# GpSimd instead of VectorE makes the marks of each edge's column in a four-layer graph network kernel

## The chip, the cores and the metric

The kernel runs on one core of a Trainium2 chip. The metric is the device time of one execution in microseconds (us), without profiling. Before the change it is 4020.64 us, the median of three runs (4017.7 to 4024.07 us). A core has a matrix engine (TensorE, PE in the profile), a vector engine (VectorE, DVE), a scalar engine (ScalarE, ACT), GpSimd (POOL) and SyncE (SP), which here only starts transfers. Each engine works through its own list of instructions in order; they wait for each other by semaphores. Transfers with a list of row numbers (indirect DMAs) are issued by GpSimd.

## The reference

There are 100,000 nodes with 16 features each and 50,000 edges. Four layers follow each other; each normalizes the node features, takes for every edge the features of one of its ends, makes a message of 16 numbers from them, and adds the messages up at the other end:

```python
edge_index = jnp.stack([src, dst])
h = relu(layernorm(x))
x = x + _L0_gnn_ref(h, edge_index, edge_weight, ...)   # message: h[src] * weight; summed at dst
h = relu(layernorm(x))
x = x + _L1_gnn_ref(h, edge_index, edge_attr_2, ...)   # 16 small products, weighted by hat functions
h = relu(layernorm(x))
x = x + _L2_gnn_ref(h, edge_index, edge_attr_8, ...)   # two edge convolutions, one in each direction
h = relu(layernorm(x))
x = x + _L3_gnn_ref(h, edge_attr_8, ...)               # message, sum, and an update of every node
```

Layers 0 and 2 gather by `src` and sum by `dst`; layers 1 and 3 the other way round.

## The kernel before

**Tiles.** A node's number is split in three: its partition (one of 128), its block of 16 columns, and its column in that block. The edges are first sorted by block, once for each of the two directions, and written as records (21 or 13 numbers each) into a table in device memory (`place(0)` and `place(1)`, line 489: 391 indirect transfers each, of 128 edges). A record holds the number of the row to gather, the partition (field `LO`) and the column in the block (field `HI`) of the node that receives the message, and the edge's attributes.

**An edge stage.** Each layer has one edge stage (`edges(l)` in the programs of VectorE and ScalarE). It goes over 55 groups of 8 tiles; a tile is 128 edges, one on each partition. For a group g:

- SyncE fetches the records of the group into `rec[g % 4]` (line 394). For group g + 4 it first waits until VectorE has made `spread` of group g and ScalarE `at_lo` of group g.
- GpSimd waits for the record (`rec_in`) and for the buffer `rows[g % 4]`, then issues 8 indirect transfers, one a tile, which gather 128 rows of 16 features (line 507).
- ScalarE makes from `LO` the 0/1 matrix `at_lo` of each edge's partition (lines 859 and 863).
- VectorE makes the message `raw` (`messages(g)`), partly from products of TensorE. In it `columns(g)` (line 1213) compares the numbers 0 to 15 with field `HI` for all 8 tiles at once: one comparison of 128x128, which leaves a 1 at the edge's column in `at_hi[g % 2]`.
- VectorE multiplies `at_hi` by `raw` into `spread` (line 1218, 128x2048).
- TensorE multiplies `at_lo` by `spread` tile by tile (line 586; in layer 3 line 582). This sums the tile's messages by partition and column.
- VectorE adds tile after tile to a running sum (`run`, line 1238, 8 instructions of 128x256 a group), and SyncE writes the group's 1 MB of running sums to device memory (line 401). `run` of group g - 1 stands behind `spread` of group g.

**Order.** The order on every engine is written out by hand. GpSimd's list is: a few masks, `place(0)`, the 440 gathers of layer 0, `place(1)`, and the 440 gathers of each of layers 1, 2 and 3, then the additions of the last stage, the node update (line 531). Between the edge stages lie node stages, in which the sums are read back and the features normalized; GpSimd waits there for the stored table of features (`store`). The node stage of layer 1 runs on the other engines while GpSimd issues `place(1)`.

**Buffers.** `rec` and `rows` are four deep (`RING`), `at_hi`, `at_lo`, `raw` and `spread` two deep. `iota16` holds the numbers 0 to 15; VectorE makes it once at the start (line 1336).

Of the kernel before, what the change touches and what calls it, by code (L numbers as in the profile page):

```python
# [4 lines left out]
P = 128  # L5
N, E, D = 100000, 50000, 16
# [4 lines left out]
BC = 16  # L11
# [25 lines left out]
G = 8  # L37
GROUPS = T // G
RING = 4
# [25 lines left out]
def build_gnn(nc, x_in, src_in, dst_in, attr2_in, attr8_in, attr8_rev_in, ew_in, w0_in, slw_in, w1_in,  # L65
# [4 lines left out]
    ALU, ACT, AX = mybir.AluOpType, mybir.ActivationFunctionType, mybir.AxisListType  # L70
# [5 lines left out]
    with ctx:  # L76
        def sb(name, shape, dt=f32):
            return ctx.enter_context(nc.sbuf_tensor(name, shape, dt))

        def sem(name):  # L80
            return ctx.enter_context(nc.semaphore(name))
# [14 lines left out]
        iota1 = sb("iota1", [P, P])  # L96
        iota16 = sb("iota16", [P, BC])
# [5 lines left out]
        rec = [sb(f"rec{k}", [P, G * FD]) for k in range(RING)]  # L103
        keep = [sb(f"keep{s}", [P, T]) for s in range(2)]
        last = [sb(f"last{s}", [P, NBS], i32) for s in range(2)]
        small = sb("small", [P, 5 * CH])
        at_hi = [sb(f"at_hi{p}", [P, G * BC]) for p in range(2)]
        hats = [sb(f"hats{p}", [P, G * 8]) for p in range(2)]
        rowmask = sb("rowmask", [P, 8])
        eps = sb("eps", [P, 1])  # L110
# [46 lines left out]
        spread = [work[:, 2048 + i * G * BW:2048 + (i + 1) * G * BW] for i in range(2)]  # L157
# [7 lines left out]
        def late(words):  # L165
# [67 lines left out]
        w4_ready = sem("w4_ready")  # L233
        stored = sem("stored")
        dve_step = sem("dve_step")

        names = ("taken", "outer", "bandT", "bandS", "prod", "used", "preact", "silu", "hats", "hatsraw",
                 "abs", "lo", "spread", "summed", "run")
        lacks = [("outer", "bandT", "bandS", "prod", "used", "preact", "silu", "hats", "hatsraw"),
                 ("taken", "preact", "silu"),  # L240
                 ("taken", "outer", "preact", "silu", "hats", "hatsraw"),
# [4 lines left out]
        rec_in = [sem(f"rec{k}") for k in range(RING)]  # L246
# [13 lines left out]
        def v3(ap, f=D):  # L260
            return ap.rearrange("p (u f) -> p u f", f=f)
# [10 lines left out]
        FIELDS = [FD, FS]  # L272
        ORDER = [0, 1, 0, 1]
        LO, HI, ROW = [D_LO, S_LO], [D_HI, S_HI], [D_SRC, S_DST]

        def field(l, k, f, n=1):

            F = FIELDS[ORDER[l]]
            return v3(rec[k][:, 0:G * F], F)[:, :, f:f + n]

        def turns(g, n):

            return g // n + 1

        def past(l, k, n):

            return l * ((GROUPS - k + n - 1) // n)

        def fetched(l, g):

            return 16 * (past(l, g % RING, RING) + turns(g, RING))
# [163 lines left out]
        def _(pool):  # L455
# [24 lines left out]
            def place(s):  # L480

                F, nat = FIELDS[s], (natD, natS)[s]
                pool.wait_ge(zeroed[s], 16)
                pool.wait_ge(copied, 6)
                for v in range(VS):
                    pool.wait_ge(places[s], v + 1)
                    for u in range(v * GS, min(v * GS + GS, NAT)):
                        n = REST if u == ET else P
                        pool.indirect_dma_start(  # L489
                            out=rec_by[s].ap(), out_offset=bass.IndirectOffsetOnAxis(ap=pos[s][0:n, u:u + 1], axis=0),  # L490
                            in_=nat[0:n, u * F:(u + 1) * F], in_offset=None).then_inc(placed[s], 16)

            place(0)
            for l in range(4):
                e = ed[l]
                used = e[("taken", "outer", "bandT", "bandT")[l]]
                F, f = FIELDS[ORDER[l]], ROW[ORDER[l]]

                pool.wait_ge(nd[l]["store"], 16 * NCH)
                for g in range(GROUPS):  # L500
                    k = g % RING
                    pool.wait_ge(rec_in[k], fetched(l, g))
                    if g >= RING:

                        pool.wait_ge(used, g - RING + 1)
                    for u in range(G):
                        pool.indirect_dma_start(  # L507
                            out=rows[k][:, u * D:(u + 1) * D], out_offset=None, in_=table.ap(),
                            in_offset=bass.IndirectOffsetOnAxis(
                                ap=rec[k][:, u * F + f:u * F + f + 1].bitcast(i32), axis=0))\  # L510
                            .then_inc(gath[k], 16)
                if l == 0:
                    place(1)

# [478 lines left out]
        def _(dve):  # L993
            V = nc.vector
            own = Steps(dve, dve_step)
# [210 lines left out]
            def edges(l):  # L1206
                s, e = ORDER[l], ed[l]
                acc = accs[l]

                def columns(g):  # L1210

                    dve.wait_ge(rec_in[g % RING], fetched(l, g))
                    own.did(V.tensor_tensor(v3(at_hi[g % 2][:, :], BC), iota16[:, None, :].to_broadcast([P, G, BC]),
                                            field(l, g % RING, HI[s]).to_broadcast([P, G, BC]), ALU.is_equal))

                def spread_out(g):
                    par = g % 2
                    V.tensor_tensor(spread[par].rearrange("p (u c f) -> p u c f", c=BC, f=D),  # L1218
                                    v3(at_hi[par][:, :], BC)[:, :, :, None].to_broadcast([P, G, BC, D]),
                                    v3(raw[par])[:, :, None, :].to_broadcast([P, G, BC, D]), ALU.mult)\  # L1220
                        .then_inc(e["spread"], 1)

# [32 lines left out]
                def messages(g):  # L1255
                    k, par = g % RING, g % 2
                    if l == 0:
                        dve.wait_ge(gath[k], gathered(l, g))
                        V.tensor_tensor(v3(raw[par]), v3(rows[k][:, :]),
                                        field(l, k, D_EW).to_broadcast([P, G, D]), ALU.mult).then_inc(e["taken"], 1)  # L1260
                        columns(g)
                        dve.wait_ge(e["taken"], g + 1)
                        own.did(V.tensor_tensor(v3(raw[par]), v3(raw[par]),
                                                w0[:, None, :].to_broadcast([P, G, D]), ALU.mult))
                    elif l == 1:
                        columns(g)
                        dve.wait_ge(e["prod"], g + 1)
                        V.tensor_tensor(prod[:, 0:512].rearrange("p (u o a) -> p u o a", o=D, a=4),
# [64 lines left out]
                run(GROUPS - 1)  # L1333

            dve.wait_ge(masks, MASKS)
            own.did(V.tensor_scalar(iota16[:, :], iota1[:, 0:BC], -1.0, None, ALU.add))
            dve.wait_ge(cleared, CLEARED)
            dve.wait_ge(ids_in, IDS)
            keys(0)
# [9 lines left out]
            for l in range(4):  # L1349
                nodes(l)  # L1350
                if l == 2:
                    dve.wait_ge(w4_psum, 1)
                    for v in range(8):
                        k = V.tensor_scalar(W4[:, v * 256:(v + 1) * 256].rearrange("p (k i) -> p i k", k=D),
                                            v3(psR[:, 0:256]), rowmask[:, v:v + 1], NORM_LIN, ALU.mult, ALU.mult)
# [31 lines left out]
            for j, (b0, nb) in enumerate(PARTS):  # L1387
# [4 lines left out]
                k = V.scalar_tensor_tensor(xs, psK[:, o:o + nb * P], NORM_LIN, xs, ALU.mult, ALU.add)  # L1392
# [30 lines left out]
```

## Time and profile before

| what | us |
|---|---|
| median of three runs without profiling | 4020.64 |
| the profiled execution, its span (the page gives no other time of its own) | 4874.8 |
| GpSimd busy in it | 2760.8 (57%) |
| VectorE busy in it | 2768.7 (57%) |
| TensorE busy in it | 2006.0 (41%) |
| ScalarE busy in it | 1193.8 (24%) |

The profiled execution took 854 us longer than the median run. In a row of the profile the busy time of an engine stands first, then the mean of one instruction in ns, then the time that the engine sat idle just before such instructions, with what ended the wait. "issue" means that the engine waited for nothing that the profile shows, "remote" that the trace shows a wait but not who released it. A `DMA_INDIRECT` row of GpSimd is the time in which GpSimd makes the transfer's descriptors, not the time in which data moves.

### The profile page before, as it was taken

To read this page: it belongs to the slowest core of one execution; us is meant where nothing else is said; L and a number is where in the kernel's file an instruction comes from. 1 tells how busy PE (TensorE), PEld (TensorE's weight loads), DVE (VectorE), ACT (ScalarE), POOL (GpSimd) and SP (SyncE) were. 2 spreads that over 40 slices of the span, in tenths; PEclk is the share of its full clock that TensorE was granted. 3 is DMA by queue.
4 is the path that set the end of the run, shared out by engine and by line. 5 is a ranking of instruction groups with operands and counts; after the bars stand their busy time and mean duration, and the time that the engine had idled before them with its cause. 6 is when DMAs were issued, how large, how long until landed. Compare 5 with 4: busy or idle time off the path is not lost.

```text
span 4874.8 us, 28541 instructions
## 1 busy us (share of the span) xinstructions
PE 2006.0 (41%) x7574; PEld 1399.7 (29%) x7574; DVE 2768.7 (57%) x4103; ACT 1193.8 (24%) x2921; POOL 2760.8 (57%) x2767
## 2 busy tenths in 40 slices
PE   1200124434310002444443066666623554546998
PEld 0000013323200002333332044444412443434444
DVE  9108425545412403555557766677684565656988
ACT  0000113223221102333333233333322222221111
POOL 4777755655677775555551255555505555553786
PEclk6555556667655556777776577777766776778999
DMA  5000212322301101222225122222342222223010
GB/s 157 9 8 15 66 51 98 99 80 98 78 25 50 57 22 37 82 87 86 86 78 118 65 71 88 80 87 82 88 136 62 82 87 77 83 81 88 31 34 27
DMA packets 192773, 345.55 MB, mean 71 GB/s; under 512 B 81018, under 2 KB 159466, under 8 KB 164067
## 3 DMA queue, kind: packets, MB, share of 16 engines
q1 hardware_dynamic: 103104, 287.51, 16.0%
q0 software_dynamic: 81344, 21.38, 6.2%
q10 hardware_dynamic: 8164, 34.85, 1.9%
q8 instruction: 61, 1.00, 0.1%
q14 instruction: 100, 0.82, 0.1%
HBM read 66.26 MB, written 277.24 MB: 70 GB/s over the span
## 4 chain that ended last, share of the span: by engine, by line
DVE 26%; another core or an unknown queue 23%; issue 19%; PE 16%; POOL 11%; ACT 2%; SPq 2%; ACTq 1%; DMA 1%; DVEq 0%; POOLq 0%
POOL edges_by_dst L489 8%; DVE natS L1238 7%; PE psK L586 5%; PE psX L733 4%; PE psK L582 4%; DVE work L1238 3%; DVE work L1218 3%; DVE natD L1238 2%; POOL natD L531 1%; PE psX L644 1%; DVE psX L1291 1%; DVE natD L1283 1%; SPq L436 1%; SPq L437 1%
## 5 line engine op out<-in xcount | busy, mean ns | idle before, releaser
L507 POOL DMA_INDIRECT rows<-table,rec x1760 | 1679.9, 955 | 1661.6 <-issue 513.3
L586 PE MATMUL psK<-work 128*128 128x256 f32 x2640 | 832.8, 478 | 698.5 <-issue 389.1
L586 PEld LDWEIGHTS psK<-work 128*128 128x128 f32 x2640 | 629.7, 248 | 878.5 <-issue 585.1
L1238 DVE SCALAR_TENSOR_TENSOR natS<-natS,keep,psK 128x256 f32<-128x256 f32 x1069 | 513.6, 480 | 336.9 <-remote 246.8
L859 ACT ACTIVATE work<-iota,rec 128x128 f32<-128x128 f32 x1760 | 539.3, 393 | 638.7 <-remote 341.2
L1218 DVE TENSOR_TENSOR work<-at_hi,psX 128x2048 f32<-128x2048 f32 x220 | 502.4, 2284 | 4.3 <-ACT psX L904 0.4
L489 POOL DMA_INDIRECT edges_by_dst<-natD,pos x391 | 388.9, 995 | 171.0 <-issue 128.3
L489 POOL DMA_INDIRECT edges_by_src<-natS,pos x391 | 394.3, 1008 | 127.4 <-issue 127.4
L733 PE MATMUL psX<-natD,work 128*128 128x512 f32 x784 | 349.6, 598 | 17.6 <-DMA work<-scan_by_column 9.5
L582 PE MATMUL psK<-work 128*128 128x128 f32 x1760 | 303.0, 352 | 126.1 <-DVE work L1218 80.1
L582 PEld LDWEIGHTS psK<-work 128*128 128x128 f32 x1760 | 292.5, 264 | 190.2 <-DVE work L1218 127.9
L531 POOL TENSOR_TENSOR natD<-natS 128x512 f32<-128x512 f32 x196 | 244.6, 1266 | 138.5 <-DVE natS L1368 138.4
L628 PE MATMUL psX<-natD 64*128 64x288 f32 (+1 forms) x440 | 137.3, 709 | 377.4 <-ACT natD L881 249.4
L1238 DVE SCALAR_TENSOR_TENSOR work<-work,keep,psK 128x256 f32<-128x256 f32 x385 | 185.1, 481 | 170.6 <-remote 120.7
L1368 DVE TENSOR_TENSOR natS<-psX,h 128x1024 f32<-128x1024 f32 x196 | 239.2, 1221 | 35.9 <-PE psX L733 35.9
L863 ACT ACTIVATE work<-work,one 128x1024 f32<-128x1024 f32 x220 | 253.3, 1151 | 10.9 <-remote 2.8
L659 PE MATMUL psX<-natD 128*128 128x128 f32 x440 | 81.2, 341 | 376.5 <-ACT natD L873 259.4
L653 PE MATMUL psX<-ident,natD 128*128 128x128 f32 x220 | 35.8, 287 | 444.3 <-issue 439.1
L733 PEld LDWEIGHTS psX<-natD,work 128*128 128x128 f32 x784 | 143.8, 191 | 188.2 <-issue 108.9
L763 ACT ACTIVATE work<-h 128x1792 f32<-128x1792 f32 x35 | 59.3, 1694 | 550.6 <-DVE h L1128 543.5
L659 PEld LDWEIGHTS psX<-natD 128*128 128x128 f32 x440 | 68.7, 238 | 390.1 <-ACT natD L873 270.4
L1238 DVE SCALAR_TENSOR_TENSOR natD<-natD,keep,psK 128x256 f32<-128x256 f32 x196 | 94.2, 481 | 145.3 <-remote 113.5
(157 smaller groups left out, 2404.5 us busy)
## 6 DMA issues: line engine op xcount, KB each, us to landing
scan<-natS SPq DMA_DIRECT2D x110, 1024.0 KB
scan<-natD SPq DMA_DIRECT2D x28, 1024.0 KB
scan_by_column<-work SPq DMA_DIRECT2D x28, 1024.0 KB
rows<-table,rec POOLq DMA_INDIRECT x1760
scan<-work SPq DMA_DIRECT2D x27, 1024.0 KB
scan_by_column<-natS SPq DMA_DIRECT2D x27, 1024.0 KB
table<-h ACTq DMA_DIRECT2D x28, 896.0 KB, 3.6
work<-scan SPq DMA_DIRECT2D x126, 128.0 KB, 2.1
```

The lines of the kernel that those rows point to most:

```text
L489: pool.indirect_dma_start(out=rec_by[s].ap(), out_offset=bass.IndirectOffsetOnAxis(ap=pos[s][0:n, u:u + 1], axis=0), in_=nat[0:n, u * F:(u ...
L507: pool.indirect_dma_start(out=rows[k][:, u * D:(u + 1) * D], out_offset=None, in_=table.ap(), in_offset=bass.IndirectOffsetOnAxis(ap=rec[k ...
L531: nc.gpsimd.tensor_tensor(hf, w[:, :, :, 0:8], w[:, :, :, 8:16], ALU.add).then_inc(up["half"], 1)
L582: k = nc.tensor.matmul(psK[:, o + half * P:o + (half + 1) * P], spread[par][:, o + half * P:o + (half + 1) * P], lo, start=True, stop=True)
L586: k = nc.tensor.matmul(psK[:, o:o + BW], lo, spread[par][:, o:o + BW], start=True, stop=True)
L659: a = nc.tensor.matmul(psP[0][:, m * P:(m + 1) * P], outerT[:, m * P:(m + 1) * P], W1[:, 0:P], start=True, stop=True)
L733: k = nc.tensor.matmul(psQ[q % 2][:, j * 512:(j + 1) * 512], sums_in[c % 2][two, b * P:(b + 1) * P], W4[two, m * 512:(m + 1) * 512], start ...
L859: a = S.activation(to[:, t * P:(t + 1) * P], iota1[:, :], ACT.Abs, bias=field(l, g % RING, LO[ORDER[l]])[:, t, :])
L863: S.activation(to, to, ACT.Relu, scale=-1.0, bias=one[:, :]).then_inc(e["lo"], 1)
L1218: V.tensor_tensor(spread[par].rearrange("p (u c f) -> p u c f", c=BC, f=D), v3(at_hi[par][:, :], BC)[:, :, :, None].to_broadcast([P, G, BC ...
L1238: V.scalar_tensor_tensor(acc[par][:, t * BW:(t + 1) * BW], was, keep[s][:, q * G + t:q * G + t + 1], psK[:, t * BW:(t + 1) * BW], ALU.mult ...
L1368: V.tensor_tensor(products(q)[0], psQ[q % 2].rearrange("p (u k i) -> p u k i", k=D, i=D), v3(h[:, bass.ds(c * CW + 64 * q, 64)])[:, :, Non ...
```

## The change

GpSimd now makes the marks of the columns. Behind each of its gathers stands a comparison of 128x16 for the tile of that gather, so 8 in a group and 1760 in all. VectorE's comparison of 128x128, one a group and 220 in all, is gone; in its place VectorE waits for a new semaphore `columns`, which counts GpSimd's comparisons. `at_hi` has four buffers, one for each of `rec` and `rows`. GpSimd waits once, ahead of its first gather, until VectorE has made `iota16`.

```diff
-        at_hi = [sb(f"at_hi{p}", [P, G * BC]) for p in range(2)]
+        at_hi = [sb(f"at_hi{k}", [P, G * BC]) for k in range(RING)]
...
+        iota_ready = sem("iota_ready")
...
         names = ("taken", "outer", "bandT", "bandS", "prod", "used", "preact", "silu", "hats", "hatsraw",
-                 "abs", "lo", "spread", "summed", "run")
+                 "abs", "lo", "spread", "summed", "run", "columns")
...
-                F, f = FIELDS[ORDER[l]], ROW[ORDER[l]]
+                F, f, h_at = FIELDS[ORDER[l]], ROW[ORDER[l]], HI[ORDER[l]]
+                if l == 0:
+                    pool.wait_ge(iota_ready, 1)
...
                             in_offset=bass.IndirectOffsetOnAxis(
                                 ap=rec[k][:, u * F + f:u * F + f + 1].bitcast(i32), axis=0))\
                             .then_inc(gath[k], 16)
+                        nc.gpsimd.tensor_scalar(
+                            at_hi[k][:, u * BC:(u + 1) * BC], iota16[:, :],
+                            rec[k][:, u * F + h_at:u * F + h_at + 1], None, ALU.is_equal)\
+                            .then_inc(e["columns"], 1)
...
                 def columns(g):
 
-                    dve.wait_ge(rec_in[g % RING], fetched(l, g))
-                    own.did(V.tensor_tensor(v3(at_hi[g % 2][:, :], BC), iota16[:, None, :].to_broadcast([P, G, BC]),
-                                            field(l, g % RING, HI[s]).to_broadcast([P, G, BC]), ALU.is_equal))
+                    dve.wait_ge(e["columns"], G * (g + 1))
...
-                                    v3(at_hi[par][:, :], BC)[:, :, :, None].to_broadcast([P, G, BC, D]),
+                                    v3(at_hi[g % RING][:, :], BC)[:, :, :, None].to_broadcast([P, G, BC, D]),
...
-            own.did(V.tensor_scalar(iota16[:, :], iota1[:, 0:BC], -1.0, None, ALU.add))
+            V.tensor_scalar(iota16[:, :], iota1[:, 0:BC], -1.0, None, ALU.add).then_inc(iota_ready, 1)
```

GpSimd's list at the start of layer 0 was the following; `n0_store` is the stored table of features and `rec0` to `rec3` are the records in the four buffers.

```order
47 L507 DMA rows<-table,rec 128x16 [waits rec0,n0_store]
48 L507 DMA rows<-table,rec 128x16 x7
49 L507 DMA rows<-table,rec 128x16 [waits rec1]
50 L507 DMA rows<-table,rec 128x16 x7
51 L507 DMA rows<-table,rec 128x16 [waits rec2]
52 L507 DMA rows<-table,rec 128x16 x7
```

After the change the same place reads:

```order
47 L510 DMA rows<-table,rec 128x16 [waits rec0,n0_store,iota_ready]
48 L515 TENSOR_SCALAR at_hi<-iota,rec 128x16
49 L510 DMA rows<-table,rec 128x16
50 L515 TENSOR_SCALAR at_hi<-iota,rec 128x16
51 L510 DMA rows<-table,rec 128x16
52 L515 TENSOR_SCALAR at_hi<-iota,rec 128x16
```

Between every two gathers there now stands a comparison, and no wait has been added inside a group.

VectorE's list for one group in the middle of layer 0 was the following; `gath0` is the landed gather, `e0_taken` VectorE's own step before, `out1` a landed write of running sums, `e0_summed` TensorE's sums.

```order
707 L1259 TENSOR_TENSOR psX<-rows,rec 128x128 [waits gath0]
708 L1213 TENSOR_TENSOR at_hi<-iota,rec 128x128 [waits rec0]
709 L1263 TENSOR_TENSOR psX<-psX,w 128x128 [waits e0_taken]
710 L1218 TENSOR_TENSOR work<-at_hi,psX 128x2048 [waits dve_step]
711 L1238 SCALAR_TENSOR_TENSOR work<-natD,keep,psK 128x256 [waits e0_run,out1,e0_summed]
712 L1238 SCALAR_TENSOR_TENSOR work<-work,keep,psK 128x256 [waits e0_run] x3
```

After the change a group there reads:

```order
627 L1264 TENSOR_TENSOR psX<-rows,rec 128x128 [waits gath0]
628 L1268 TENSOR_TENSOR psX<-psX,w 128x128 [waits e0_taken,e0_columns]
629 L1223 TENSOR_TENSOR work<-at_hi,psX 128x2048 [waits dve_step]
630 L1243 SCALAR_TENSOR_TENSOR work<-natD,keep,psK 128x256 [waits e0_run,out1,e0_summed]
631 L1243 SCALAR_TENSOR_TENSOR work<-work,keep,psK 128x256 [waits e0_run] x3
```

The comparison is gone from VectorE, and the next instruction also waits for GpSimd's marks of the group.

## Rows read from the trace of the kernel before

**Rows 1.** The page's busy time, share of the span and instructions, by engine.
```profile
PE 2006.0 (41%) x7574; PEld 1399.7 (29%) x7574; DVE 2768.7 (57%) x4103; ACT 1193.8 (24%) x2921; POOL 2760.8 (57%) x2767
```

**Rows 2.** GpSimd's groups of indirect transfers: count, busy, mean, idle before, releasers.
```profile
L507 POOL DMA_INDIRECT rows<-table,rec x1760 | 1679.9, 955 | 1661.6 <-issue 513.3 <-DMA rec<-edges_by_src 450.3 <-DMA rec<-edges_by_dst 397.1
L489 POOL DMA_INDIRECT edges_by_src<-natS,pos x391 | 394.3, 1008 | 127.4 <-issue 127.4
L489 POOL DMA_INDIRECT edges_by_dst<-natD,pos x391 | 388.9, 995 | 171.0 <-issue 128.3 <-DVE pos L1104 42.7
```

**Rows 3.** GpSimd in order of time in layer 0: start, us, instruction, idle before.
```profile
933.85 0.94 POOL L507 DMA_INDIRECT rows<-table,rec  x1 [0.30 <-issue]
935.09 0.95 POOL L507 DMA_INDIRECT rows<-table,rec  x1 [0.30 <-issue]
948.46 0.94 POOL L507 DMA_INDIRECT rows<-table,rec  x1 [12.42 <-DMA rec<-edges_by_dst]
```

**Rows 4.** SyncE and VectorE in order of time in the same wait.
```profile
935.65 0.48 DVE L1238 SCALAR_TENSOR_TENSOR natD<-work,keep,psK 128x256 f32<-128x256 f32 x1 [14.63 <-remote]
...
944.03 2.29 DVE L1218 TENSOR_TENSOR work<-at_hi,psX 128x2048 f32<-128x2048 f32 x1
...
946.35 0.32 SPq L394 DMA_DIRECT2D rec<-edges_by_dst  x1
951.04 2.29 DVE L1218 TENSOR_TENSOR work<-at_hi,psX 128x2048 f32<-128x2048 f32 x1
```

**Rows 5.** VectorE between two waits in layers 1, 2 and 3.
```profile
2418.01 2.28 DVE L1218 TENSOR_TENSOR work<-at_hi,psX 128x2048 f32<-128x2048 f32 x1
2426.41 2.28 DVE L1218 TENSOR_TENSOR work<-at_hi,psX 128x2048 f32<-128x2048 f32 x1
...
3080.95 2.29 DVE L1218 TENSOR_TENSOR work<-at_hi,psX 128x2048 f32<-128x2048 f32 x1
3091.33 2.29 DVE L1218 TENSOR_TENSOR work<-at_hi,psX 128x2048 f32<-128x2048 f32 x1
...
4163.18 2.28 DVE L1218 TENSOR_TENSOR work<-at_hi,psX 128x2048 f32<-128x2048 f32 x1
4173.71 2.28 DVE L1218 TENSOR_TENSOR work<-at_hi,psX 128x2048 f32<-128x2048 f32 x1
...
4192.26 2.28 DVE L1218 TENSOR_TENSOR work<-at_hi,psX 128x2048 f32<-128x2048 f32 x1
4202.29 2.28 DVE L1218 TENSOR_TENSOR work<-at_hi,psX 128x2048 f32<-128x2048 f32 x1
```

**Rows 6.** GpSimd in layer 2: the starts of two groups.
```profile
3113.99 0.94 POOL L507 DMA_INDIRECT rows<-table,rec  x1 [8.47 <-DMA rec<-edges_by_dst]
3124.39 0.94 POOL L507 DMA_INDIRECT rows<-table,rec  x1 [0.69 <-DMA rec<-edges_by_dst]
```

**Rows 7.** VectorE's comparison and its neighbour in order of time, layer 0.
```profile
950.31 0.29 DVE L1259 TENSOR_TENSOR psX<-rows,rec 128x128 f32<-128x128 f32 x1
950.51 0.29 DVE L1213 TENSOR_TENSOR at_hi<-iota,rec 128x128 f32<-128x128 f32 x1
950.72 0.29 DVE L1263 TENSOR_TENSOR psX<-psX,w 128x128 f32<-128x128 f32 x1
```

**Rows 8.** GpSimd's small instructions at the start, in order of time.
```profile
1.10 0.10 POOL L458 MEMSET rowmask<- 128x8 f32 x1
1.14 0.09 POOL L459 MEMSET padmask<- 128x2 bf16 x1
1.17 0.20 POOL L460 MEMSET allones<- 128x128 bf16 x1
...
2.56 0.18 POOL L472 TENSOR_SCALAR_AFFINE_SELECT padmask<-padmask 128x2 bf16<-128x2 bf16 x1
2.70 0.18 POOL L474 TENSOR_SCALAR_AFFINE_SELECT rowmask<-rowmask 128x8 f32<-128x8 f32 x1
2.95 0.19 POOL L477 TENSOR_SCALAR_AFFINE_SELECT rowmask<-rowmask 128x8 f32<-128x8 f32 x1
```

## The prediction

> **What bounds the kernel now.** I read first the page's busy line [rows 1]: GpSimd and VectorE are both busy for 57% of the span, so shares alone do not say which sets the pace. The second view is the list of GpSimd's groups [rows 2]. The 1760 gathers are busy for 1679.9 us at 955 ns each, and idle before them is 1661.6 us in three kinds: 513.3 us "issue", 397.1 + 450.3 = 847.4 us waiting for a record, and the rest waiting for the node stages. The third view is GpSimd in order of time [rows 3]: a gather starts every 1.25 us (0.95 busy and 0.30 of "issue" before the next), 8 x 1.25 = 10.0 us a group, until it waits 12.42 us for a record.
>
> Why is that record late? [Rows 4] show it: VectorE waits 14.63 us inside `run` on something the trace doesn't name, only then makes the next `spread` at 944.03, SyncE fetches the record at 946.35 behind it, and GpSimd goes on at 948.46. So in the profiled execution GpSimd is at times held up by VectorE's chain. I hold those hold-ups for an addition of the profiled execution, for one reason of number: its span is 4874.8 us, the timed runs take 4020.64 us, and 4874.8 - 847.4 = 4027.4 us, within 0.2% of the median. Taking GpSimd's waits for records away, and nothing else, gives the timed runs.
>
> Without them, VectorE's chain can go faster than GpSimd in two layers. Between hold-ups one group takes it 951.04 - 944.03 = 7.0 us in layer 0 [rows 4], 8.4 us in layer 1, 10.4 us in layer 2, and in layer 3 once 10.5 and once 10.0 us, for which I take 10.2 [rows 5]. Layer 2 shows the same from the other side: GpSimd starts a group 10.4 us after the one before, with 0.69 us of wait at the record in place of 0.30 [rows 6]. So GpSimd's 10.0 us is the bound in layers 0 and 1 with 3.0 and 1.6 us to spare, and in layers 2 and 3 the chain of VectorE and TensorE is ahead of it by 0.4 and 0.2 us a group.
>
> **What is removed.** VectorE's 220 comparisons. A record is 0.29 us long but the neighbours start 0.20 us apart [rows 7], so each frees 0.20 us. In layers 0 and 1 that is worth nothing: GpSimd's list covers it. In layers 2 and 3 it takes the chain from 10.4 and 10.2 to 10.2 and 10.0 us. Alone, this would give (0.2 + 0.2) x 55 = 22 us.
>
> **What is added.** 1760 comparisons of 128x16 on GpSimd, one between every two gathers. Call the cost of one c; a group then takes GpSimd 10.0 + 8c. GpSimd has no such instruction behind a gather in this trace, so c is bounded from the nearest rows [rows 8]. From below: two small memsets start 0.03 to 0.04 us apart, so c = 0.03 if small instructions flow into one another. Below nothing of extra time: the 0.30 us of "issue" between two gathers might hold the comparison whole, c = 0. From above: the record of a 128x8 select is 0.19 us, and if a second gap of 0.30 us comes with it, c = 0.49. I take c = 0.19: the select is an instruction that reads and writes a small tile, as the comparison does, and gathers do not flow into one another [rows 3], so I expect its whole record behind the gather, with the 0.30 us of gap paid once as now.
>
> [...]
>
> With c = 0.19 a group takes GpSimd 10.0 + 1.52 = 11.52 us, and GpSimd is the bound in all four layers:
>
> - layers 0 and 1: 11.52 - 10.0 = 1.52 us x 110 groups = 167 us
> - layer 2: 11.52 - 10.4 = 1.12 us x 55 = 62 us
> - layer 3: 11.52 - 10.2 = 1.32 us x 55 = 73 us
>
> Together 302 us. Layer 0's share isn't hidden later: `place(1)` stands behind it in GpSimd's list, and the first gather of layer 1 behind that.
>
> **The new waits.** VectorE now waits for the marks of group g before its second instruction in layer 0 and before the products in the others. The last mark of a group is made 0.2 us behind the last gather's descriptors, and VectorE has to wait for that gather's data anyhow, which comes later; cost nothing. If the marks were late, `spread`, TensorE's sums and the record of group g + 4 would be queued behind them. The wait for `iota16` is over long before the first gather at 567 us (`place(0)` covers it). The four buffers can't hold GpSimd up: a record g + 4 is only fetched after `spread` g.
>
> **The sum.** Against the profiled execution without its waits for records: 4027.4 + 302 = 4329 us. The median lies 7 us below that rebuilt time, so I forecast 4020.6 + 302 = 4322, rounded to 4320 us. The same formula at the ends: at c = 0.03 layers 0 and 1 gain 0.24 us a group, layer 2 loses 0.16 us of its old time and layer 3 stands about still: 55 x (0.24 + 0.24 - 0.16 + 0.04) = 20 us, 4040 us (4058 at c = 0.04). At c = 0.49 a group takes 13.92 us: 55 x (3.92 x 2 + 3.52 + 3.72) = 829 us, 4850.
>
> **Rivals.**
>
> - *Small instructions flow (c up to 0.10).* For it: the memsets [rows 8]. Against: no gather flows into the next. Time 4040 to 4164, by the memsets themselves 4058.
> - *Two gaps (c from 0.35).* For it: the "issue" of 0.30 us stands before every indirect transfer, gathers and scatters alike (513.3 / 1760 and 127.4 / 391 [rows 2]), and might come before and behind a comparison. Against: small instructions of GpSimd's own show no gap between each other. Time 4620 to 4850.
> - *The gap hides the comparison, and VectorE's 0.20 us is gained.* The place is the 0.30 us between two gathers; the price is c = 0 and it decides as long as the comparison fits in the gap. Then layers 0 and 1 stay at 10.0 us and layers 2 and 3 fall to 10.2 and 10.0: 4020.6 - 22 = 3999 us, faster. For it: 0.19 is less than 0.30. Against: the gap is there when a wait has let GpSimd's queue fill up, so it looks like work of GpSimd itself and not like idle room.
> - *The waits for records are real in timed runs too.* Then GpSimd has 847.4 / 220 = 3.85 us a group to spare, 1.52 us fit in, and the change does nothing: about 4020 us. For it: the waits stand in the only trace there is. Against: 854 us of difference between profiled and timed would then have to come from elsewhere, and no other group of idle time has that size.
>
> **Chances.** My forecast's mechanism, with c from 0.10 to 0.35: 0.58. Small instructions flow: 0.14. Two gaps: 0.12. Hidden in the gap: 0.07. Waits real: 0.09. A difference below about 0.2% (8 us) can't be told from none. Faster: the hidden case, 0.07. Same: the fourth case, 0.09, and 0.02 of the flowing case, 0.11. Slower: the rest, 0.82. The likeliest case alone spans c = 0.10 to 0.35, from 0.80 x 2 + 0.40 + 0.60 = 2.6 us x 55 = 143 us to 2.8 x 2 + 2.4 + 2.6 = 10.6 us x 55 = 583 us: 4164 to 4604 us. The range takes in the flowing case and the case of no change, and stops at c near 0.36: 4012 to 4620 us; left out are the faster case and most of the two gaps.
>
> **What would show it right or wrong.** In the profile after: the distance from one gather to the next in a group is 1.44 us (right), 1.25 (hidden), 1.3 (flowing), or over 1.6 (two gaps). GpSimd's busy time rises by 1760 x 0.19 = 334 us. VectorE's groups between hold-ups stand no closer than GpSimd's in layer 0. The waits for records shrink or go; if the profiled span less those waits isn't close to the timed median again, my reading of the profiled execution is wrong. A wait of VectorE on GpSimd's marks, instead of on the gather's data, would show the new semaphore costing time of its own.

## The result and the profile after

The changed kernel takes 4544.01 us (median of four runs, 4542.68 to 4545.11), the kernel before 4019.7 us (4017.7 to 4024.07). The ratio is 1.131, 95% interval 1.1296 to 1.1324: slower by 524 us. The forecast was 4320 us, range 4012 to 4620.

The page of the kernel after, its busy line, its chain and the two groups of GpSimd:

```profile
PE 2067.8 (46%) x7574; PEld 1447.1 (32%) x7574; DVE 2743.8 (60%) x3883; ACT 1182.2 (26%) x2921; POOL 3485.6 (77%) x4527
POOL 72%; issue 14%; PE 6%; DVE 6%; DMA 1%; SPq 1%; ACT 0%; POOLq 0%; DVEq 0%
L510 POOL DMA_INDIRECT rows<-table,rec x1760 | 1797.7, 1021 | 571.5 <-issue 291.2
L515 POOL TENSOR_SCALAR at_hi<-iota,rec 128x16 f32<-128x16 f32 x1760 | 638.2, 363 | 59.8
```

Against [rows 1], GpSimd's busy share went from 57% to 77%, but the 57% is a share of a span that the timed runs don't have. In the second profile of the kernel before (e6 below) it is 68%, and GpSimd makes up 53% of the chain that ended last, against 72% now. Against [rows 2], the waits for records are gone from the first releasers: of 571.5 us of idle time before gathers 291.2 is "issue", and GpSimd's own list accounts for the rest (272.6 us of it the two waits for the table of features).

GpSimd in order of time in layer 0 after the change (start, us, instruction, idle before), to be read beside [rows 3]:

```profile
999.62 1.01 POOL L510 DMA_INDIRECT rows<-table,rec  x1 [0.16 <-issue]
1000.67 0.35 POOL L515 TENSOR_SCALAR at_hi<-iota,rec 128x16 f32<-128x16 f32 x1
1001.19 1.03 POOL L510 DMA_INDIRECT rows<-table,rec  x1 [0.17 <-issue]
1002.25 0.35 POOL L515 TENSOR_SCALAR at_hi<-iota,rec 128x16 f32<-128x16 f32 x1
```

From one gather to the next it is now 1.57 us in place of 1.25. Three things changed, not one: the gather's own record is 1.02 us long instead of 0.95; the comparison's record is 0.35 us; and the gap before the next gather is 0.17 us instead of 0.30. So a comparison costs 1.57 - 1.25 = 0.32 us.

Since the first trace of the kernel before had waits that the timed runs don't have, I profiled that kernel a second time (e6 below) and take the layers from there. The rows give for each layer the gathers' count, their shortest, median and longest record in ns, and the start of the first and of the last; what stands behind the semicolon isn't needed here. First the kernel before, second profile:

```profile
L507 POOL DMA_INDIRECT rows<-table,rec x440: 943/947/1067, 552.5 to 1102.6; - x147
L507 POOL DMA_INDIRECT rows<-table,rec x440: 943/947/1429, 1610.0 to 2166.1; - x147
L507 POOL DMA_INDIRECT rows<-table,rec x440: 942/947/1199, 2335.5 to 2916.9; - x147
L507 POOL DMA_INDIRECT rows<-table,rec x440: 943/947/975, 3044.6 to 3594.0; - x147
```

Then the kernel after:

```profile
L510 POOL DMA_INDIRECT rows<-table,rec x440: 992/1018/1134, 550.8 to 1239.9; - x147
L510 POOL DMA_INDIRECT rows<-table,rec x440: 987/1014/1509, 1750.0 to 2460.9; - x147
L510 POOL DMA_INDIRECT rows<-table,rec x440: 994/1018/1081, 2623.4 to 3316.6; - x147
L510 POOL DMA_INDIRECT rows<-table,rec x440: 994/1014/1033, 3429.4 to 4117.6; - x147
```

Last start less first start gives the edge stage of each layer; divided by 54.9 groups (439 steps of 8) it gives the time of a group.

| stage | before, us (a group) | after, us (a group) | more |
|---|---|---|---|
| layer 0 | 550.1 (10.02) | 689.1 (12.55) | 139.0 |
| layer 1 | 556.1 (10.13) | 710.9 (12.95) | 154.8 |
| layer 2 | 581.4 (10.59) | 693.2 (12.63) | 111.8 |
| layer 3 | 549.4 (10.01) | 688.2 (12.54) | 138.8 |
| all between and around them | 1788.6 | 1761.6 | -27.0 |
| span | 4025.6 | 4543.0 | 517.4 |

Layers 0 and 3 show the plain price, 139 / 440 = 0.32 us for each comparison. Layer 1 pays 16 us more than that, layer 2 pays 27 us less. The last line but one is the time from the last gather of a layer to the first of the next and the two ends: with GpSimd slower, the engines behind it have less left to do when it issues its last gather of layers 1, 2 and 3 (169.4 us became 162.5, 127.7 became 112.8, and the end 431.6 became 425.4). The last `spread` of the layer shows it: its end came 22.8, 27.5 and 21.4 us behind the start of that gather before, and comes 15.9, 12.4 and 15.1 us behind it now.

### The profile page after: what moved, and what is told of

Its sections match the earlier page's. It is cut to its first block, busy times and chain, and to the rows that moved or that the text cites. A ratio compares the mean times of both kernels' runs of the same rounds, so it can differ in the third digit from the quotient of the medians.

```text
span 4543.0 us, 30299 instructions
## 1 busy us (share of the span) xinstructions
PE 2067.8 (46%) x7574; PEld 1447.1 (32%) x7574; DVE 2743.8 (60%) x3883; ACT 1182.2 (26%) x2921; POOL 3485.6 (77%) x4527
## 4 chain that ended last, share of the span: by engine, by line
POOL 72%; issue 14%; PE 6%; DVE 6%; DMA 1%; SPq 1%; ACT 0%; POOLq 0%; DVEq 0%
POOL rows L510 40%; POOL at_hi L515 14%; POOL edges_by_src L490 8%; POOL edges_by_dst L490 8%; PE psX L740 5%; POOL natD L538 1%; DVE h L1135 1%; DVE natS L1373 1%; DVE psX L1132 1%; POOL x L534 1%; POOL x L526 1%; PE psK L721 0%; SPq L437 0%; DVE natS L1243 0%; DVE h L1174 0%
## 5 line engine op out<-in xcount | busy, mean ns | idle before, releaser
L510 POOL DMA_INDIRECT rows<-table,rec x1760 | 1797.7, 1021 | 571.5 <-issue 291.2
L593 PEld LDWEIGHTS psK<-work 128*128 128x128 f32 x2640 | 665.2, 259 | 895.4 <-issue 766.1
L515 POOL TENSOR_SCALAR at_hi<-iota,rec 128x16 f32<-128x16 f32 x1760 | 638.2, 363 | 59.8
L490 POOL DMA_INDIRECT edges_by_src<-natS,pos x391 | 377.8, 966 | 127.1 <-issue 127.1
L1264 DVE TENSOR_TENSOR psX<-rows,rec 128x128 f32<-128x128 f32 x55 | 16.5, 300 | 547.3 <-DMA rows<-table,rec 547.3
L589 PEld LDWEIGHTS psK<-work 128*128 128x128 f32 x1760 | 272.5, 248 | 84.2 <-issue 77.8
L589 PE MATMUL psK<-work 128*128 128x128 f32 x1760 | 283.0, 335 | 5.5 <-DVE work L1223 5.5
L660 PEld LDWEIGHTS psX<-ident,natD 128*128 128x128 f32 x220 | 28.1, 164 | 721.2 <-issue 509.3
L635 PE MATMUL psX<-natD 64*128 64x288 f32 (+1 forms) x440 | 178.2, 906 | 69.5 <-ACT natD L885 49.4
L678 PE MATMUL psX<-ident,rows 128*128 128x128 f32 x110 | 41.7, 380 | 366.4 <-DMA rows<-table,rec 366.4
L1255 DVE TENSOR_TENSOR natD<-rows,hats 128x512 f32<-128x512 f32 x55 | 38.1, 693 | 274.8 <-DMA rows<-table,rec 274.8
```

The costliest lines, as they stand in the source:

```text
L490: pool.indirect_dma_start(out=rec_by[s].ap(), out_offset=bass.IndirectOffsetOnAxis(ap=pos[s][0:n, u:u + 1], axis=0), in_=nat[0:n, u * F:(u ...
L510: pool.indirect_dma_start(out=rows[k][:, u * D:(u + 1) * D], out_offset=None, in_=table.ap(), in_offset=bass.IndirectOffsetOnAxis(ap=rec[k ...
L515: nc.gpsimd.tensor_scalar(at_hi[k][:, u * BC:(u + 1) * BC], iota16[:, :], rec[k][:, u * F + h_at:u * F + h_at + 1], None, ALU.is_equal)\
L589: k = nc.tensor.matmul(psK[:, o + half * P:o + (half + 1) * P], spread[par][:, o + half * P:o + (half + 1) * P], lo, start=True, stop=True)
L593: k = nc.tensor.matmul(psK[:, o:o + BW], lo, spread[par][:, o:o + BW], start=True, stop=True)
```

## The experiments

All ratios are to the kernel before on the same chip, in whose sets it took 4020 to 4026 us.

**e1, the comparisons of a group together behind its gathers.**

```diff
                     for u in range(G):
                         pool.indirect_dma_start(...)
-                        nc.gpsimd.tensor_scalar(at_hi[k][...u...], ...)
+                    for u in range(G):
+                        nc.gpsimd.tensor_scalar(at_hi[k][...u...], ...)
```

> GpSimd's 8 comparisons of a group stand together behind the group's eighth gather instead of one behind each gather; nothing else differs from the changed kernel (4544 us). Theory A, every comparison costs GpSimd's list the same 0.32 us wherever it stands (1.57 us from gather to gather after, 1.25 before): 4544 us within 0.3%, a group of layer 0 still 12.5 us. Theory B, the price is that of changing between gather and comparison, and comparisons in a row flow into each other as the small memsets did: the seven in a row cost about 0.15 us each, a group takes 10.0 + 0.3 + 7 x 0.15 = 11.4 us, and the kernel about 4544 - 1.1 x 220 = 4300 us.

Measured: 4500.43 us, ratio 1.1193 (1.1174 to 1.1212). GpSimd at the end of a group of layer 0:

```profile
1017.38 0.94 POOL L510 DMA_INDIRECT rows<-table,rec  x1 [0.30 <-issue]
1018.62 0.94 POOL L510 DMA_INDIRECT rows<-table,rec  x1 [0.30 <-issue]
1019.60 2.38 POOL L516 TENSOR_SCALAR at_hi<-iota,rec 128x16 f32<-128x16 f32 x8
1022.14 1.03 POOL L510 DMA_INDIRECT rows<-table,rec  x1 [0.16 <-issue]
```

Eight comparisons in a row take 2.38 us, 0.30 us each. They do not flow into each other; theory B falls, and theory A is off by a twelfth: a group takes 12.35 us in layer 0 in place of 12.55, so of the 0.32 us about 0.02 belongs to the change between gather and comparison. Only the gather right behind the eight is 1.03 us long.

**e3, a comparison with a constant.** The number of the record is not read.

```diff
-                            rec[k][:, u * F + h_at:u * F + h_at + 1], None, ALU.is_equal)\
+                            3.0, None, ALU.is_equal)\
```

> Each comparison of GpSimd compares with the constant 3 instead of the edge's number in the record; the marks are therefore not those of the edges. Same count, shape and place. Theory A, the instruction costs GpSimd its dispatch and not its operands: 4544 us, a comparison's record stays at 0.36 us. Theory B, the number read from memory, one for each partition, is what makes the record 0.36 us where the 128x8 select had 0.19: the record falls to about 0.20 us, gather to gather to 1.41 us, and the kernel to about 4544 - 0.16 x 1760 = 4262 us.

Measured: 4407.05 us, ratio 1.0964 (1.0946 to 1.0982).

```profile
L515 POOL TENSOR_SCALAR at_hi<-iota 128x16 f32<-128x16 f32 x1760 | 511.2, 290 | 43.5
```

Between the two theories. Reading the number costs 0.07 us of the record (363 to 290 ns) and (1.131 - 1.0964) x 4020 = 139 us of the kernel; a comparison with a constant still costs 0.24 us from gather to gather.

**e4, no marks at all after the first two groups of a layer.** This bounds what any move of VectorE's comparison can bring.

```diff
                     dve.wait_ge(rec_in[g % RING], fetched(l, g))
+                    if g >= 2:
+                        return
                     own.did(V.tensor_tensor(v3(at_hi[g % 2][:, :], BC), ...
```

> The kernel before, with VectorE's comparison made only in the first two groups of each layer and left out in the other 53 (the marks of the later groups are stale). GpSimd has no comparison. Theory A, GpSimd's gathers bound layers 0 and 1, and VectorE's chain bounds layers 2 and 3 by 0.2 to 0.4 us a group: 0.2 x 106 = 21 us are gained, 3999 us. Theory B, GpSimd's gathers are the bound in all four layers: 4020 us within 0.2%. Theory C, VectorE's chain is the bound everywhere: 0.2 x 212 = 42 us gained, 3977 us. In both A and B the profiled execution shows waits for records again, and the span less those waits is within 0.5% of the timed median.

Measured: 4018.63 us, ratio 0.9997 (0.9987 to 1.0006): the number of theory B. The trace that the expectation wanted, with waits for records, didn't come: they are 43.4 us in all. Layers 0 and 2:

```profile
L507 POOL DMA_INDIRECT rows<-table,rec x440: 940/944/1031, 550.5 to 1098.8; - x147
L507 POOL DMA_INDIRECT rows<-table,rec x440: 938/944/1168, 2329.1 to 2908.3; - x147
```

Layer 2 takes 579.2 us against 581.4, and layer 0 548.3 against 550.1. The comparison on VectorE was hidden everywhere, in layer 2 too. There theory B has the mechanism wrong: at 10.55 us a group GpSimd isn't the bound of that layer.

**e5, two comparisons behind each gather**, the first into a spare tile.

```diff
+                        nc.gpsimd.tensor_scalar(spare[k][...u...], ...).then_inc(e["columns"], 1)
                         nc.gpsimd.tensor_scalar(at_hi[k][...u...], ...).then_inc(e["columns"], 1)
```

> Behind each gather GpSimd makes two comparisons of 128x16, the first into a spare tile that nobody reads; VectorE waits for both. Theory A, each comparison costs the same 0.32 us: the second adds 0.32 x 1760 = 563 us, 5107 us in all. Theory B, a comparison behind a comparison flows into it and costs 0.15 us: 264 us more, 4808 us. Theory C, the first comparison was partly hidden in the gap of 0.30 us between gathers (its record of 0.36 us cost only 0.32) and the second has no gap to hide in: 0.36 to 0.50 us, 5180 to 5420 us.

Measured: 5057.58 us, ratio 1.2579 (1.2558 to 1.26). The second comparison costs (1.2579 - 1.131) x 4020 = 510 us, 0.29 us each. This is theory A with the 0.30 us of e1.

**e6, the kernel before once more.** No edit.

> The kernel before, unchanged, profiled once more. The prediction read the waits for records in its first trace (847 us in a span of 4875 us) as an addition of that profiled execution. Theory A, that is right and it was this one execution: the span is now within 1% of 4020 us, the waits for records are under 60 us, and a group of layer 0 takes 10.0 us. Theory B, profiling this kernel always adds them (gathers 1.25 us apart are too dense for the records): the span is again above 4700 us.

Measured: one run of 4027.31 us, and the span of its profile is 4025.6 us.

```profile
L507 POOL DMA_INDIRECT rows<-table,rec x1760 | 1675.7, 952 | 867.8 <-issue 526.1 <-DMA table<-h 294.9 <-DMA rec<-edges_by_dst 41.8
```

Theory A. Of the 847.4 us of waits for records in [rows 2] the second profile shows 45.5 us (41.8 in this row and 3.7 for the other table of records); issue (526.1 against 513.3) and the table (294.9 us) are as they were. The waits belonged to that one profiled execution. What made them there stays open; in none of the twelve other profiles of this case are they above 49 us.

Of the 45.5 us, 38.0 are in layer 2. The chain of the same trace between 2335 and 2920 us, the edge stage of layer 2, tells what sets the pace there:

```profile
by line: PE psK L586 39.6%; DVE natS L1238 34.2%; PE psX L644 15.6%; issue 3.7%; DVE x L1310 2.8%; POOL rows L507 2.4%; DMA table<-h 0.7%; DMA rows<-table,rec 0.4%; DVE work L1218 0.4%; DVE psX L1291 0.2%; PE psX L628 0.2%; PE psK L605 0.2%
```

It is TensorE's sums (line 586), VectorE's running sums (line 1238) and a product of TensorE (line 644). GpSimd has 2.4% of it, and VectorE's comparison (line 1213) isn't in it.

**e7, a memset in place of the comparison.** The marks are all zero.

```diff
-                        nc.gpsimd.tensor_scalar(at_hi[k][...u...], ...)
+                        pool.memset(at_hi[k][:, u * BC:(u + 1) * BC], 0.0).then_inc(e["columns"], 1)
```

> In place of each comparison GpSimd clears the 128x16 marks (a memset, nothing is read); the marks are all zero. Theory A, any instruction of GpSimd behind a gather has a price near the comparison's with a constant (0.24 us from gather to gather): 4350 to 4450 us. Theory B, the price is that of the instruction itself, as the prologue of the trace shows it, where memsets of 128x8 start 0.03 to 0.04 us apart: 1760 x 0.04 = 70 us less what layer 2 absorbs (30 to 50 us), 4040 to 4060 us. Theory C, between the two: its record of about 0.10 us is paid in full: 0.10 x 1760 - 45 = 131 us, 4150 us.

Measured: 4032.26 us, ratio 1.0019 (1.0009 to 1.0028). None of the three: it costs 8 us in all.

```profile
899.97 0.95 POOL L510 DMA_INDIRECT rows<-table,rec  x1 [0.18 <-issue]
900.91 0.14 POOL L515 MEMSET at_hi<- 128x16 f32 x1
901.22 0.95 POOL L510 DMA_INDIRECT rows<-table,rec  x1 [0.18 <-issue]
```

The next gather still starts 1.25 to 1.26 us behind the last: the memset stands whole in the gap of 0.30 us.

**e8, the comparisons together behind the fourth gather.**

```diff
                             .then_inc(gath[k], 16)
+                        if u == 3:
+                            for t in range(G):
+                                nc.gpsimd.tensor_scalar(at_hi[k][...t...], ...)
```

> The 8 comparisons of a group stand together behind its fourth gather. Behind the eighth they gave 4500 us, with 12.35 us a group in layers 0, 2 and 3 but 12.73 in layer 1, where some comparisons last 0.7 to 0.8 us while VectorE multiplies two operands from the same memory (the outer product of rows and hats). Theory A, GpSimd's comparison is held while VectorE works on two operands from that memory: behind the fourth gather the two don't meet, layer 1 falls to 12.35 us a group, 4500 - 0.38 x 55 = 4479 us. Theory B, layer 1's extra time has another cause (its narrower records, its chain): layer 1 stays at 12.7 us and the kernel at 4500 us.

Measured: 4506.86 us, ratio 1.1203 (1.1184 to 1.1222), not apart from e1. Layer 1 takes 12.68 us a group (12.73 in e1), layer 0 12.35 as in e1. The number is theory B's, but the trace says why: now a gather is met in place of a comparison. VectorE and GpSimd in layer 1:

```profile
2006.37 0.69 DVE L1257 TENSOR_TENSOR natD<-rows,hats 128x512 f32<-128x512 f32 x1 [4.55 <-DMA rows<-table,rec]
2006.43 1.45 POOL L510 DMA_INDIRECT rows<-table,rec  x1 [0.30 <-issue]
```

A gather that starts 0.06 us into VectorE's outer product lasts 1.45 us instead of 0.94. Of the 46 gathers that start inside the product in this trace, the 40 that start 0.05 to 0.21 us into it last 1.30 to 1.46 us; five that start 0.02 to 0.03 us into it, and one at 0.60 us, have their usual length. So a gather is held as a comparison is, and e8 could not tell the two theories apart as I had set it up. A memset isn't held: in layer 1 of e7's trace 20 of them start inside the product, and none lasts over 0.14 us.

**e9, one wide comparison a group**, of 128x128 with a constant.

```diff
+                    nc.gpsimd.tensor_scalar(at_hi[k][:, :], iota1[:, :], 3.0, None, ALU.is_equal)\
+                        .then_inc(e["columns"], G)
```

> GpSimd makes one comparison of 128x128 with the constant 3 behind a group's eighth gather in place of eight of 128x16; the marks are not those of the edges. Theory A, the price is mostly fixed for each instruction: 0.28 + 112 elements x 0.8 ns (the slope between the 128x8 and the 128x128 select of the trace) = 0.37 us, plus 0.15 us for the dearer gather behind it, 0.5 x 220 = 110 us less 30 absorbed in layer 2: 4100 us. Theory B, it goes by elements, eight times the width costs what eight comparisons cost: 4407 us.

Measured: 4114.28 us, ratio 1.0226 (1.0207 to 1.0246).

```profile
L515 POOL TENSOR_SCALAR at_hi<-iota 128x128 f32<-128x128 f32 x220 | 123.1, 560 | 4.8
```

Theory A. Eight times the width takes 560 ns against 290 in e3, 2.4 ns for each further element; the group takes 10.57 us in layer 0. The price is mostly for the instruction: eight of 128x16 with a constant cost 388 us of the kernel (e3), one of 128x128 costs 91. Both compare with a constant. One wide comparison with the edges' own numbers, which is the work that VectorE did, was not run on GpSimd.

**e10, one operand of layer 1's outer product in PSUM.** The kernel's tiles lie in two memories of the core, SBUF and PSUM. Of those named here only `psX` and `psK` are in PSUM. ScalarE writes a copy of the hat factors into a free part of `psX`.

```diff
+        hatsP = [psX[:, 1024 + p * G * 8:1024 + (p + 1) * G * 8] for p in range(2)]
...
+                    S.activation(hatsP[g % 2], hats[g % 2][:, :], ACT.Relu, scale=-1.0, bias=one[:, :])\
+                        .then_inc(e["hats"], 1)
...
-                                    hat_of(k, 1)[:, :, :, None].to_broadcast([P, G, 4, D]), ALU.mult)\
+                                    hatsP[k % 2].rearrange("p (u c n) -> p u c n", c=2, n=4)[:, :, 1, :]
+                                    [:, :, :, None].to_broadcast([P, G, 4, D]), ALU.mult)\
```

> The changed kernel (4544 us), in which ScalarE also writes a copy of the hat factors into a free part of psX, and VectorE's outer product of layer 1 reads the factors there: one operand from SBUF and one from PSUM instead of two from SBUF. Its moment doesn't move. Theory A, an instruction of GpSimd that starts while VectorE reads two operands from SBUF is held until VectorE is through (comparisons of 0.67 to 0.81 us in layer 1, a gather of 1.49): the comparisons of layer 1 fall to 0.35 us like the others, its groups from 12.95 to 12.55 us, and the kernel by 0.4 x 55 = 22 us to 4522 us. Theory B, it is not the operands but the landing of the gather or something else at that moment: layer 1 stays at 12.95 us and the kernel at 4544 us.

Measured: 4534.7 us, ratio 1.1261 (1.1246 to 1.1276) against the changed kernel's 1.131 (1.1296 to 1.1324): 20 us faster by the ratios. Layer 1's gathers, and the same moment in the middle of layer 1:

```profile
L511 POOL DMA_INDIRECT rows<-table,rec x440: 991/1014/1040, 1749.4 to 2437.6; - x147
```

```profile
2001.09 0.69 DVE L1259 TENSOR_TENSOR natD<-rows,psX 128x512 f32<-128x512 f32 x1 [3.66 <-DMA rows<-table,rec]
2001.25 0.36 POOL L516 TENSOR_SCALAR at_hi<-iota,rec 128x16 f32<-128x16 f32 x1
```

Theory A. Layer 1 takes 688.2 us in place of 710.9, 12.53 a group, as layers 0 and 3 do. VectorE's product still takes 0.69 us. The comparison starts inside it as before and lasts 0.36 us; 47 comparisons of layer 1 start inside such a product, and that is the longest of them.

**e11, two memsets behind each gather**, of 128x8 each; the marks are all zero.

```diff
-                        nc.gpsimd.tensor_scalar(at_hi[k][...u...], ...)
+                        pool.memset(at_hi[k][:, u * BC:u * BC + 8], 0.0).then_inc(e["columns"], 1)
+                        pool.memset(at_hi[k][:, u * BC + 8:(u + 1) * BC], 0.0).then_inc(e["columns"], 1)
```

> Two memsets of 128x8 behind each gather in place of the comparison; the marks are all zero. One memset of 128x16 there cost nothing: it stood in the 0.30 us between two gathers, and the next gather started 1.25 us after the last as before. Theory A, what stands in the gap costs nothing as long as its end is 0.17 us ahead of the next gather: two memsets that start 0.03 to 0.04 us apart end at 0.17 us and cost 0.03 us at most, 1760 x 0.03 less what layer 2 absorbs, 4025 to 4065 us. Theory B, each further instruction costs a dispatch of about 0.15 us: 0.15 x 1760 - 45 = 219 us, 4245 us.

Measured: 4047.07 us, ratio 1.005 (1.0035 to 1.0066), 20 us.

```profile
901.27 0.95 POOL L510 DMA_INDIRECT rows<-table,rec  x1 [0.15 <-issue]
902.21 0.13 POOL L515 MEMSET at_hi<- 128x8 f32 x1
902.26 0.13 POOL L516 MEMSET at_hi<- 128x8 f32 x1
902.53 0.95 POOL L510 DMA_INDIRECT rows<-table,rec  x1 [0.15 <-issue]
```

Theory A. The pair ends 0.17 us behind the gather, the next gather starts 0.15 us later, at 1.26 to 1.27 us from the last. The gap is full.

**e12, the kernel before with e10's copy.** The edit is that of e10.

> The kernel before, with the copy of the hat factors in PSUM and nothing else. In the second profile of the kernel before some gathers of layer 1 last 1.11 to 1.40 us in place of 0.95 while VectorE makes the outer product, and a group takes 10.13 us in layer 1 where it takes 10.02 in layer 0. Theory A (held by two operands in SBUF): layer 1 falls to 10.02 us a group, 6 us in all, 4014 us against 4020 us, at the edge of what can be told. Theory B: no change, 4020 us.

Measured: 4019.96 us against 4026.01 us on the same chip, ratio 0.9985 (0.9976 to 0.9994). Layer 1's gathers:

```profile
L508 POOL DMA_INDIRECT rows<-table,rec x440: 941/947/1045, 1609.4 to 2158.9; - x147
```

Layer 1 takes 549.5 us in place of 556.1, and no gather of it is longer than 1.05 us. Theory A, at the edge of what can be told: by its interval the gain is 2 to 10 us, and the 6.6 us of layer 1 in the trace agree. Of the versions with the right marks this is the one that beats both kernels.

## Why the prediction was right, and where a term was off

The direction, the engine that sets the pace and the path of the cost were right. The size was not: 302 us were forecast and 524 came. The range held them because it was wide: its upper end stands for a price of 0.36 us a comparison, and the price came out at 0.32 where 0.19 was taken. Two of its own signs missed as well. A gather came 1.57 us behind the last, not 1.44, and GpSimd's busy time rose by 761 us (from 2724.9 in e6 to 3485.6), not by 334: 638 are the comparisons and 122 the gathers, whose records got longer.

**GpSimd's gathers are the bound; the timed runs don't have the waits of the first trace.** Right in layers 0, 1 and 3, and e6 shows it: span 4025.6 us, 10.02 us a group in layer 0. The rival that the waits are real falls with it.

**The chain of VectorE and TensorE sets the pace, by 0.4 us a group in layer 2 and by 0.2 in layer 3.** Read from quick pairs in the disturbed trace [rows 5]. Wrong for layer 3, which takes 10.01 us (e6); too small for layer 2, which takes 10.59. And the 22 us that were to come from the removed comparison don't exist: with all but 8 of the 220 comparisons left out the ratio is 0.9997 (e4). In layer 2 that chain does set the pace, but the comparison isn't a link of it: e6's trace has TensorE's sums, the running sums and a product of TensorE in it, for 89% of the stage.

**The price of a comparison, c = 0.19 us.** This is the term that was mis-sized; it is 0.32 us. I took the record of a 128x8 select [rows 8] and left gather and gap as they stood. What the runs put in its place:

- the record itself is 0.35 us, of which 0.07 is the number read for each partition (e3)
- the gather behind a comparison lasts 0.07 us longer, 1.02 against 0.95 us
- the gap of 0.30 us shrinks to 0.03 before the comparison and 0.17 before the gather

0.35 + 0.07 + 0.03 + 0.17 - 0.30 = 0.32 us. Against 0.19, the record is 0.16 us longer than I had it; the 0.07 of the gather was at nothing in my sum, without a reason; and I had the gap paid in full, where 0.10 us of it is saved. The last error works against the other two, which is luck: with the right record alone and the gap paid in full c would have been 0.35. The bound from above, 0.49, held. Why a gather behind a comparison lasts longer stays open; behind a memset it doesn't (0.95 us, e7).

**The sum.** By the same formula with c = 0.32, and layer 2 and 3 bases of 10.4 and 10.2 us, it would have been 55 x (2.56 x 2 + 2.16 + 2.36) = 530 us, against 524 measured. So the mechanism carries the number. That it comes so close is in part luck, since smaller terms were missed or mis-sized and nearly cancel: the collision in layer 1 (+16 us beyond what it already cost before), the slack of layers 2 and 3 (27 + 0 us where 22 + 11 were counted), and the shorter ends of the layers (-27).

**The rivals.** "Small instructions flow" holds for memsets (e7, e11) and not for the comparison (e1). "The gap hides it" was the right mechanism for the wrong instruction: a memset that ends 0.13 us behind the gather is all but free (8 us for 1760 of them, e7), while the comparison, 0.35 us long, saves 0.10 us of the gap and pays the rest, and 0.07 us in the gather behind it. "Two gaps" is half right: there are two gaps, but together they are 0.20 us, less than the one before. My argument against the hidden case, that the gap is GpSimd's own work, is only half true: 0.15 to 0.18 us of it stayed empty before the next gather whatever stood there (the changed kernel, e1, e7, e9, e11), and the rest could be used.

**The new wait.** Right. VectorE waits for the gather's data, as said, and all but never for the marks:

```profile
DVE psX L1264 <- DMA rows<-table,rec: 547.3, 55, 246.3
DVE natD L1255 <- DMA rows<-table,rec: 274.8, 55, 16.3
DVE natD L1303 <- POOL at_hi L515: 6.1, 2, 4.4
```

The columns are us in total, number of waits and the longest; the third row and one wait of 0.5 us in layer 0 are all of VectorE's waiting for GpSimd's marks, so the new semaphore costs 6.6 us at most.

**The comparison beside a rule.** For GpSimd's elementwise work the Trainium skill ("GPSIMD Engine Reference", section 3.1, "Elementwise — side-by-side cycle accounting") gives about 1.8 cycles an element as the best case of a tight loop, 1.5 ns at its 1.2 GHz. The comparison doesn't reach it: 128x128 with a constant takes 560 ns (e9) and 128x16 with a constant 290 ns (e3), 2.4 ns for each further element. For this comparison the measurement decides.

## What to carry to other kernels

An engine that issues indirect gathers back to back is full although their records cover only 0.95 of each 1.25 us: count the distance from start to start, not the records. Comparisons moved there pay for each instruction far more than for their width: with a constant, one of 128x128 cost 0.55 us a group (e9) and eight of 128x16, at 0.24 us each, cost 1.9 (e3). Before moving work off an engine, leave it out altogether once: here that run (e4) shows that nothing could be gained.

## What the hardware showed that was not expected

**A gather or a comparison of GpSimd that starts while VectorE reads two operands from SBUF is held.** In layer 1 the outer product of `rows` and `hats` (both in SBUF, 0.69 us) starts on the landing of a group's last gather, mostly 2.4 to 2.6 us behind the start of that gather's record, and so nearly always meets GpSimd at the same place: 50 of layer 1's comparisons start inside it, and all 50 last 0.63 us or more. The changed kernel in layer 1:

```profile
2009.95 0.69 DVE L1255 TENSOR_TENSOR natD<-rows,hats 128x512 f32<-128x512 f32 x1 [4.18 <-DMA rows<-table,rec]
2010.08 0.76 POOL L515 TENSOR_SCALAR at_hi<-iota,rec 128x16 f32<-128x16 f32 x1
2010.56 2.28 DVE L1223 TENSOR_TENSOR work<-at_hi,psX 128x2048 f32<-128x2048 f32 x1
2011.01 1.03 POOL L510 DMA_INDIRECT rows<-table,rec  x1 [0.16 <-issue]
```

The comparison that starts 0.13 us into it lasts 0.76 us in place of 0.35, until 0.2 us after VectorE is done. The product of 128x2048 behind it, with one operand in PSUM, holds nobody: the next gather takes 1.03 us beneath it. Gathers are held in the same way (1.45 us in e8), memsets are not (e7). A gather that is under way when VectorE's product starts isn't held: the one under way at 2009.95 had its usual length (1.01 us). It isn't only this product: in layer 2 of the changed kernel 21 comparisons last 0.46 to 0.63 us, each beside VectorE's addition of `x` and `bias`, whose operands are both in SBUF too (line 1317; some start up to 0.07 us before it), and e10, which leaves that addition as it is, still has them. With one operand in PSUM the hold is gone (e10, 20 us; e12, 6 us). The Trainium skill has the rule for the comparison ("SBUF — State Buffer", "Who interferes with whom"): a VectorE instruction with two SBUF inputs contends with a GpSimd instruction that reads SBUF, not with one that only writes it, and the shared ports are an exclusive lock. The rows agree for the comparison, which reads, and for the memset, which only writes. For the making of a transfer's descriptors the section infers that such a product leaves it alone; here a gather was held by 0.51 us (1.45 in place of 0.94) and the comparison by 0.41, and the measurement decides.

**A first profile can carry 850 us that the kernel doesn't have**, and look whole while doing so. Its span against the timed median was the sign that gave it away.
